# Storing and returning a block of node features in pieces, and splitting the first chunk of a wide product, in a four-layer graph network

## The reference, cut to what matters

```python
h = gat_conv(x, src, dst, W1, att_src1, att_dst1, b1, concat=True)   # 4 heads -> 3125 x 1024
# graph_norm:
mean = h.mean(axis=0); sh = h - ms * mean
var = (sh * sh).mean(axis=0)
h = relu(w * sh / sqrt(var + 1e-5) + b)
out = gat_conv(h, src, dst, W2, att_src2, att_dst2, b2, concat=False)  # 1024 -> 256
x = x + out
```

## Time and profile before

| | |
|---|---|
| median of three timed runs | 3726.94 us (3725.66 to 3728.96) |
| the profiled execution | 3722.49 us, span of the trace 3720.8 us |
| TensorE busy | 3368.7 us, 91% |
| VectorE busy | 2306.9 us, 62% |
| ScalarE busy | 840.3 us, 23% |
| GpSimd busy | 802.8 us, 22% |
| DMA | 572.59 MB, mean 154 GB/s |
| chain that ended last | PE 42%, DVE 7%, issue 4%, DMA 1%, ACT 1% |
| stages of the last layer | steps 0 to 7 about 1936 to 3245 us, results of step 7 to 3263, wide product to 3387, steps 8 and 9 to the end |

### The profile page before, as it was taken

One profiled execution on the slowest core, in us unless ns is written; L12 is line 12 of the kernel. 1 busy time (PEld: TensorE's weight loads), 2 busy tenths in 40 slices (PEclk: granted clock), 3 DMA queues, 4 the chain that ended last, 5 costly groups with the idle time before them and its releaser, 6 DMA issues.

```text
span 3720.8 us, 34248 instructions
## 1 busy us (share of the span) xinstructions
PE 3368.7 (91%) x12633; PEld 1922.4 (52%) x12633; DVE 2306.9 (62%) x3034; ACT 840.3 (23%) x1110; POOL 802.8 (22%) x652
## 2 busy tenths in 40 slices
PE   6999857687999999999828999999999999987998
PEld 6897646564554554545524444444444444464444
DVE  9972222236011102434697888888888899868987
ACT  0103322235000000133112222222222222242222
POOL 3788888860000000000011111111111000011000
PEclk9999989898999999999959999999999999998999
DMA  9999978896443444322456555555555432274422
GB/s 349 365 282 243 271 181 227 226 258 131 141 131 124 127 139 135 96 84 62 120 168 147 117 129 118 136 132 117 136 118 131 109 96 71 84 255 145 123 62 68
DMA packets 277905, 572.59 MB, mean 154 GB/s; under 512 B 93162, under 2 KB 157440, under 8 KB 275440
## 3 DMA queue, kind: packets, MB, share of 16 engines
q1 hardware_dynamic: 139545, 432.89, 36.6%
q0 software_dynamic: 85712, 77.51, 13.3%
q10 hardware_dynamic: 52480, 60.01, 6.1%
HBM read 365.44 MB, written 204.87 MB: 153 GB/s over the span
## 4 chain that ended last, share of the span: by engine, by line
PE 42%; DVE 7%; issue 4%; DMA 1%; ACT 1%; POOL 0%; DVEq 0%; ACTq 0%; POOLq 0%
PE ps L1196 29%; PE ps L1035 3%; PE ps L1160 2%; PE ps L1229 2%; PE ps L1203 2%; DVE R L2102 2%; DVE wB L2065 1%; DVE PT L1897 1%; DVE wA L1897 1%; PE ps L988 1%; DMA den_d<-R 0%; PE ps L1231 0%; DVE PT L2065 0%; PE ps L1136 0%; PE ps L1096 0%
## 5 line engine op out<-in xcount | busy, mean ns | idle before, releaser
L1196 PE MATMUL ps<-R,B 125*128 125x500 f32 x2800 | 1094.6, 542 | 40.8 <-DVE R L2102 34.7
L1196 PEld LDWEIGHTS ps<-R,B 125*128 125x128 f32 x2800 | 504.1, 190 | 604.0 <-issue 554.2
L705 POOL DMA_INDIRECT pairs<-w x400 | 618.6, 1546 | 195.5 <-issue 105.8
L1035 PE MATMUL ps<-R,H 125*128 125x500 f32 (+1 forms) x1400 | 542.9, 542 | 15.1 <-ACT H L1285 7.6
L1412 ACT ACTIVATE R<-R,asc 125x1625 f32<-125x1625 f32 (+1 forms) x200 | 320.2, 1601 | 998.0 <-DVE R L2089 998.0
L2089 DVE SCALAR_TENSOR_TENSOR R<-H,asc 125x1625 f32<-125x1625 f32 (+1 forms) x200 | 369.0, 1846 | 152.0 <-PE ps L1203 121.4
L2102 DVE SCALAR_TENSOR_TENSOR R<-R 125x1625 f32<-125x1625 f32 (+1 forms) x250 | 445.1, 1780 | 0.0
L1035 PEld LDWEIGHTS ps<-R,H 125*128 125x128 f32 x1400 | 253.2, 191 | 283.9 <-issue 280.9
L888 PE MATMUL ps<-R,H 125*128 125x375 f32 (+1 forms) x1000 | 302.3, 449 | 100.8 <-DMA R<-pairs 100.3
L735 POOL DMA_DIRECT2D den_d<-R x138 | 119.1, 863 | 803.3 <-DVE R L2102 774.2
L1196 PE MATMUL ps<-R,H 125*128 125x500 f32 (+1 forms) x700 | 274.1, 548 | 18.6 <-DVE R L2102 16.8
(11 more groups left out here) (315 smaller groups left out, 3039.5 us busy)
## 6 DMA issues: line engine op xcount, KB each, us to landing
pairs<-R SPq DMA_DIRECT2D x25, 3200.0 KB
R<-ct_d SPq DMA_DIRECT2D x162, 406.2 KB, 3.4
R<-pairs SPq DMA_DIRECT2D x25, 2500.0 KB
R<-ct_d SPq DMA_DIRECT2D x162, 375.0 KB, 3.1
R<-wt_d SPq DMA_DIRECT2D x50, 812.5 KB, 4.4
R<-wt_d SPq DMA_DIRECT2D x50, 750.0 KB, 4.2
den_d<-R POOLq DMA_DIRECT2D x75, 312.5 KB, 5.5
den_d<-R POOLq DMA_DIRECT2D x75, 250.0 KB, 4.8
```

What stands on the lines that cost most here:

```text
L705: pool.indirect_dma_start(pairs, bass.IndirectOffsetOnAxis(ap=key_u[:, c:c + 1], axis=0), val[:, c, :], None, compute_op=ALU.add)\
L1035: last = mm(ps[:, bank, at:at + w], rows[0:Q, j, f * 128:(f + 1) * 128], TL[q % TS][0:Q, o:o + w], start=j == 0 and at == 0, stop=j == NB ...
L1196: last = mm(ps[:, bank, at:at + w], rows[0:Q, j, f * 128:(f + 1) * 128], TT[q % TR][0:Q, o:o + w], start=j == 0 and at == 0, stop=j == NB ...
```

## The change

Four edits, all in the last layer.

1. The store of X in step 0 becomes five pieces of five node blocks each (1280 columns, 5120 bytes a partition, 640 KB over 125 partitions), at the loads of units 13, 15, 17, 19 and 21. The waits on `x_out` ask for all five.
2. The return of X in step 8 becomes five pieces in the same manner, and the wait on `x_back` asks for all five.
3. The graph-norm vectors are made in two parts by one function: tiles 0 to 5 (heads 0 to 2, `GT`) right after VectorE's last unit of step 7 and ahead of step 7's results, tiles 6 and 7 after them. ScalarE takes the first square root ahead of emptying the banks of step 7, the second between tiles 5 and 6 of the first wide chunk.
4. TensorE works on the first wide chunk in two passes: tiles 0 to 5 of its four blocks, each in a bank of its own, once six tiles are normalised; then tiles 6 and 7 and the bias of the same four. Its wait for all freed auxiliary banks (`aux_free`) ahead of the wide product is left out.

```diff
+        XAT = {LCR + 7 + 2 * i: (i * 5 * D, (i + 1) * 5 * D) for i in range(NB // 5)}
+        GT = (STEPS - 2) // 2 * KT
...
                 if q == LCR + 7:
                     uv_rows(1, 0, 1, 0)
                     sp.wait_ge(S("ln_done"), 4 * NB)
+                if q in XAT:
+                    x0, x1 = XAT[q]
                     for p0, p1 in PART:
-                        sp.dma_start(x_d[p0:p1, :], Xf[p0:p1, :]).then_inc(S("x_out"), 16)
+                        sp.dma_start(x_d[p0:p1, x0:x1], Xf[p0:p1, x0:x1]).then_inc(S("x_out"), 16)
...
+                if q - STEPS * NB in XAT:
+                    x0, x1 = XAT[q - STEPS * NB]
                     for p0, p1 in PART:
-                        sp.dma_start(Xf[p0:p1, :], x_d[p0:p1, :]).then_inc(S("x_back"), 16)
+                        sp.dma_start(Xf[p0:p1, x0:x1], x_d[p0:p1, x0:x1]).then_inc(S("x_back"), 16)
...
             pe.wait_ge(S("agg_ev"), ev0[STEPS])
-            pe.wait_ge(S("aux_free"), pre2)
             pe.wait_ge(S("va_made"), 1)
+            def wide_block(n, slot, b, t0, t1):
+                for t in range(t0, t1):
+                    last = mm(ps[0:Q, n % 4, 0:D + 2], slot[:, t, b * Q:(b + 1) * Q], w32[:, t, :], start=t == 0, stop=False)
+                if t1 == CT:
+                    mm(ps[0:Q, n % 4, 0:D], ones[0:1, 0:Q], bcs[0:1, 4, :], start=False, stop=True).then_inc(S("ring_pe"), 1)
             n = 0
             for c, (n0, nn) in enumerate(WCH):
+                slot = R[:, WSLOT[c]:WSLOT[c] + CT * nn].rearrange("p (t n) -> p t n", t=CT)
+                if c == 0:
+                    pe.wait_ge(S("wide_norm"), GT)
+                    for b in range(nn // Q):
+                        ring_wait("z3", b)
+                        wide_block(b, slot, b, 0, GT)
                 pe.wait_ge(S("wide_norm"), CT * (c + 1))
                 for b in range(nn // Q):
-                    ring_wait("z3", n)
-                    for t in range(CT):
...
+                    if c:
+                        ring_wait("z3", n)
+                    wide_block(n, slot, b, 0 if c else GT, CT)
                     n += 1
...
+            act.wait_ge(S("gn_var"), 1)
+            a(aff[:, 1, 0:GT], aff[:, 0, 0:GT], ACT.Sqrt).then_inc(S("gn_std"), 1)
             evac_step(STEPS - 1, aggT[0])
-            act.wait_ge(S("gn_var"), 1)
-            a(aff[:, 1, :], aff[:, 0, :], ACT.Sqrt).then_inc(S("gn_std"), 1)
             act.wait_ge(S("gn_aff"), 1)
...
                 for t in range(CT):
+                    if c == 0 and t == GT:
+                        act.wait_ge(S("gn_var"), 2)
+                        a(aff[:, 1, GT:CT], aff[:, 0, GT:CT], ACT.Sqrt).then_inc(S("gn_std"), 1)
+                        act.wait_ge(S("gn_aff"), 2)
                     a(slot[:, t, :], slot[:, t, :], ACT.Relu, scale=aff[:, 2, t:t + 1], bias=aff[:, 3, t:t + 1])\
...
+            def norm_vectors(t0, t1, n):
+                dve.wait_ge(S("gst_made"), YN // CT * t1)
+                for t in range(t0, t1):
+                    link.mark(v_.bn_aggr(mv[:, t, :], gst[:, t, :, :].rearrange("p c s -> p (c s)")))
+                link.join()
...
             attention(0, STEPS * NB, results_in)
+            norm_vectors(0, GT, 0)
             for i in range(results(STEPS - 1)):
                 result_in(STEPS - 1, i, True)
...
+            norm_vectors(GT, CT, 1)
```

More of the change, by code:

```diff
@@ L1219, in _ @@
             pe.wait_ge(S("agg_ev"), ev0[STEPS])
-            pe.wait_ge(S("aux_free"), pre2)
             pe.wait_ge(S("va_made"), 1)
+            def wide_block(n, slot, b, t0, t1):
[3 more added lines that the diff above has]
+                    mm(ps[0:Q, n % 4, 0:D], ones[0:1, 0:Q], bcs[0:1, 4, :], start=False, stop=True).then_inc(S("ring_pe"), 1)
             n = 0
             for c, (n0, nn) in enumerate(WCH):
+                slot = R[:, WSLOT[c]:WSLOT[c] + CT * nn].rearrange("p (t n) -> p t n", t=CT)
[4 more added lines that the diff above has]
+                        wide_block(b, slot, b, 0, GT)
                 pe.wait_ge(S("wide_norm"), CT * (c + 1))
-                slot = R[:, WSLOT[c]:WSLOT[c] + CT * nn].rearrange("p (t n) -> p t n", t=CT)
                 for b in range(nn // Q):
-                    ring_wait("z3", n)
-                    for t in range(CT):
[L1229 to L1232, removed]
+                    if c:
+                        ring_wait("z3", n)
+                    wide_block(n, slot, b, 0 if c else GT, CT)
                     n += 1
@@ L1417, in evac_step @@
                 if k == 0:
-                    act.wait_ge(S("x_out"), 32)
+                    act.wait_ge(S("x_out"), 32 * len(XAT))
                 if 1 <= k < STEPS:
@@ L2067, in den_add @@
                     if k == 6:
-                        dve.wait_ge(S("x_out"), 32)
+                        dve.wait_ge(S("x_out"), 32 * len(XAT))
                     if k == STEPS + 1:
@@ L2129, in results_in @@
                     prelude_second_in(0, 1, ad_of(0, 1), 0, j - 1 - LATER)
+            def norm_vectors(t0, t1, n):
[3 more added lines that the diff above has]
+                link.join()
+                f = [aff[:, i, t0:t1] for i in range(6)]
+                w = [colw[:, i, t0:t1] for i in range(4)]
+                link(tt(f[5], mv[:, t0:t1, 0], w[0], ALU.add))
+                link(ts(f[4], w[3], -1.0, 1.0, ALU.mult, ALU.add))
+                link(tt(f[4], f[4], f[5], ALU.mult))
+                link(tt(f[4], f[4], f[4], ALU.mult))
+                stt(f[0], mv[:, t0:t1, 1], BN_EPS, f[4], ALU.add, ALU.add).then_inc(S("gn_var"), 1)
+                dve.wait_ge(S("gn_var"), n + 1)
+                link(tt(f[4], w[3], f[5], ALU.mult))
+                link(tt(f[4], f[4], w[0], ALU.subtract))
+                dve.wait_ge(S("gn_std"), n + 1)
+                link(v_.reciprocal(f[1], f[1]))
+                link(tt(f[2], f[1], w[1], ALU.mult))
+                link(tt(f[4], f[4], f[2], ALU.mult))
+                tt(f[3], w[2], f[4], ALU.subtract).then_inc(S("gn_aff"), 1)
@@ L2150, in _ @@
-            link(tt(aff[:, 2, :], aff[:, 1, :], colw[:, 1, :], ALU.mult))
-            link(tt(aff[:, 4, :], aff[:, 4, :], aff[:, 2, :], ALU.mult))
-            tt(aff[:, 3, :], colw[:, 2, :], aff[:, 4, :], ALU.subtract).then_inc(S("gn_aff"), 1)
+            norm_vectors(GT, CT, 1)
             for r in range(2 * NB):
@@ L2192, in outs_in @@
                     if j == 0:
-                        dve.wait_ge(S("x_back"), 32)
+                        dve.wait_ge(S("x_back"), 32 * len(XAT))
                     out_in(STEPS, j - 2 - LATER)
```

## The result

The changed kernel takes 3700.77 us (median of four runs, 3700.14 to 3702.42) against 3726.30 us before (four runs, 3723.51 to 3728.96): 25.5 us less. The ratio is 0.9931, with a 95% interval of 0.9919 to 0.9942. The profiled execution has a span of 3699.5 us, 21.3 us less than the 3720.8 of the earlier trace rows. The forecast was 3703 us, 23.8 us less.

A forecast was written before the change was run, and what follows sets the result against it. TensorE was taken as the bound, losing time to a late denominator sum behind step 0's store and before the wide product; gains of 10.6 + 13.2 = 23.8 us from 3726.94 gave 3703 us, range 3696 to 3715.

The forecast's parts named there:

- What bounded the kernel: TensorE, busy for 91% of the span, so time counts where it stands still or runs at its lower clock.
- both places: Attention step 0, costing 13.1 us, and the passage into the wide product, where TensorE starts after 11.54 us.
- The time that comes in step 0: Step 0: new stalls from sums behind the store's pieces, 2.5 us together (0.2 to 5.6).
- Two of the signs that the forecast named: Step 0: sums behind pieces 2 to 5 land by 7.6 us; no score wait over 1 us behind later pieces.
- the margin of 7.2 us: Step 0: a denominator sum may land 7.2 us after issue before TensorE loses anything; the usual landing is 5.3 us.
- The rule of taking turns: Step 0: DMA engines alternate between queues packet by packet; piece 1 would cost nearly nothing, part 1 be 2.1 us better.
- The return: X's return in five pieces: gain 0 and cost 0, since nothing waits for that load.
- The vectors: Before the wide product: first vectors ready at 3242.3, 3.3 us ahead of bank emptying; second ready at 3267.7; cost 0.
- The two passes: First wide chunk: four blocks end at 3280.9 instead of 3294.09, gain 13.2 us; six tiles ready 4.4 us early.
- The fixed cost of each piece: Step 0 rival, chance 0.12: each piece delays a sum 2.7 us more, 16 us for five, time 3716.6 us.
- The rival of an unfilled gap: Wide product rival, chance 0.11: the first pass doesn't fill TensorE's gap, 1.3 us remain of the tail, time 3715.0 us.
- The slower case: Step 0 rival, chance 0.02: sums behind each piece land after 14.0 us, stalls outweigh the gains, time 3735 us.

The follow-up runs named there:

- e4: The kernel before with only 8 of the 6400 columns of X stored and returned: 3715.67 us in one run.
- e9: The changed kernel run once more, unaltered: 3701.91 us, ratio to before 0.9937.
- e1: The kernel before with only the store of X split into five pieces: 3717.81 us against 3726.64, ratio 0.9977.
- e5: The changed kernel with the store's five pieces issued earlier, beside the last count tiles of the first maxima: 3700.17 us, ratio to before 0.9931.
- e10: e5 with one more edit, ScalarE's emptying of block 11 moved behind the normalising of the next chunk: 3696.16 us, ratio to before 0.9920.
- e3: The changed kernel with all five pieces of the store issued at one point, ten DMAs in a row: 3709.31 us, ratio to before 0.9952.
- e6: The changed kernel with the store in ten pieces of 640 columns, one a unit from unit 14, return unsplit: 3702.08 us, ratio to before 0.9933.
- e7: The kernel before with only the vectors of six tiles made early, TensorE still waiting for all eight tiles: 3717.47 us in one run.
- e8: The kernel before with only the two passes over the first wide chunk, all vectors made at the end: 3723.68 us in one run.

## Why the prediction was right

**What bounded the kernel.** Right at both places. The cost of the first was put at 13.1 us, and e4 without the store is 13.2 us shorter there. In all 23.8 us were forecast; the medians gave 25.5 and, with the same kernel run again as e9, 23.3.

**The time that comes in step 0.** Right in kind, and 2.5 us forecast against 3.4 measured (3.36 in waits; 9.5 us gained net, where 10.6 were forecast). e1 has 3.11 us of waits and e9, the same kernel again, 2.33, so the closeness of the sum is partly luck: two terms were off and partly cancelled. The sum behind piece 1 was put at 7.4 + 1.9 = 9.3 us and 2.1 us of stall; it landed at 8.4 and cost 1.16. Behind the score rows alone that sum took 6.8, 7.6 and 7.0 us in e4, e5 and e10, so the piece added some 1.3 us and not 1.9. The four others were put at 0.1 us each; they cost 0, 0.55, 0.44 and 1.21, 2.2 in sum instead of 0.4.

Two of the signs that the forecast named went against it there. A sum beside pieces 2 to 5 was to land by 7.6 us, and the one at 2006.25 landed after 8.5 (8.2 in e1, 8.0 in e9): piece 2 follows piece 1 after 8.7 us and not 12.5, because SP was late at piece 1 behind the score rows. It cost nothing only because the stall before had pushed TensorE's need back by 1.16 us: 7.2 + 1.16 is 8.4. And VectorE's scores waited 2.01, 2.10 and 2.85 us for the sums beside pieces 3 to 5, where none over 1 us was forecast. The sum needn't be issued behind the piece: those at 2006.25, 2020.60 and 2033.68 were issued 0.12 us ahead of it.

The other three landings were near the forecast of 7.2 us (7.2, 7.1 and 7.6). What failed is the margin of 7.2 us, taken at the one spot of the earlier trace rows where VectorE was a little ahead. After a stall TensorE starts at once on the product it waited for, so the next sums go out later against TensorE's clockwork. At 2020.60 the unit in work ended at 2033.44 - 0.55 = 2032.89, and 2032.89 - 5.55 - 2020.60 - 0.1 leaves 6.6 us. A landing of 7.2 then costs 0.6, as seen. By the same working the sum at 2046.94 had 6.4 us, and its 7.6 cost 1.2. The unit behind each stall kept its 5.75 us, as forecast.

**The rule of taking turns.** The forecast weighed the Trainium skill, "DMA: Bandwidth & Descriptors", section "Queues, rings and completion order", by which piece 1 would cost nearly nothing, where the rows said 2.1 us. It cost 1.16 us, between the two, so neither was the better guide. The forecast read the empty 2 us of the earlier trace rows as no turns beside the score rows, on weak ground: that sum was issued at 2331.45, and even the ordinary sum issued at 2067.05 moved no packet before 2069.1. The wider window bears it out all the same, since the sum beside the score rows moved none before 2335.6, 4.1 us after its issue, while the hardware queue moved 176 by 2335.5. Once both queues move packets the trace agrees with the rule, about one for one in the earlier trace rows and in e3 (126 beside 144). What holds the first packet of a sum back no run here separates.

**The return.** Nothing was forecast and nothing was found.

**The vectors.** The first vectors were forecast 3.3 us ahead of the emptying; the last operation ends at 3235.30 and the emptying starts at 3238.74, 3.4 us.

**The two passes.** Forecast 13.2 us, measured 13.7. Six tiles were ready at 3247.79 + 4.28 = 3252.07, 4.4 us ahead of TensorE, the forecast's very number. The first pass started without the 0.3 us allowed for it.

**The rivals.** The fixed cost of each piece falls with e6. It was priced by SP's wait of 2.7 us for the small DMA, which begins behind SP's own 0.39 us of issue, so the price was a little low. The rule beside it (the Trainium skill, "DMA: Bandwidth & Descriptors", section "Bandwidth", batch to 1 MiB) says how to move bytes fast; here the smaller transfers made the kernel faster, since another transfer's latency was what counted. The rival of an unfilled gap was mispriced, though it didn't come about: I let 1.3 us remain of the tail without the first pass, and e7 shows 5.2. I had forgotten that the six activations are out of the chain as well. The slower case would have needed landings of 14 us behind each piece; beside spaced pieces none passed 8.5 in step 0, and even that is over the 7.6 that the forecast allowed.

## What to carry to other kernels

A large transfer off the critical path costs what it does to the small, latency-bound transfers beside it: find the one with the smallest margin (here 1.9 us under a DMA sum), and either cut the large one into pieces below that margin and space them (unspaced, in e3, they kept more than half of the gain but not all) or, better, move it to a stretch where nothing so tight is under way. Where a gap comes from a serial chain at a stage's end, split the work by what its inputs depend on; a consumer that may start early gains little unless its producer was moved too, as e7 and e8 show with 5.2 and 0.7 us against 13.7 together. A margin read at one spot holds only for that state of the pipeline.

## What the runs showed that I had not expected

TensorE's clock can fall after a short wait. In e3, waits of 1.90 and 2.42 us were each followed by a unit of 7.45 us instead of 5.75. The wait of 2.02 us in the wide product was followed by a slow block (5.16 to 5.44 us, clock 0.69 in e9) in five profiles, e1, e3, e5, e6 and e9, and by the usual 3.75 us in the six others that have it. Waits up to 1.3 us in step 0 never cost a slow unit. So this wait of 2 us costs 2.0 or 3.7 us; what decides which was not tested. The slow block is the 1.6 us between the two values of c to d in the table of stages, and no part of what the edits did.
